# The lead and tile 0's stage of a four-engine transformer kernel in another order: solve input ahead of weight splits, tile 7's scan ahead of the router's maxima

## The reference

```python
x = _layernorm(x + _L0_attn_ref(x, ...))   # delta-rule attention, 4 heads of 32, chunks of 32 tokens
x = _layernorm(x + _L0_ffn_ref(x, ...))    # 8 experts, top two by a router, GELU, hidden 256
x = _layernorm(x + _L1_attn_ref(x, ...))   # gated linear recurrence: a scan over time
x = _layernorm(x + _L1_ffn_ref(x, ...))    # gated silu, two GELU layers of 512, output
```

```python
def body(i, a):
    row = a[..., i, :]
    upd = jnp.einsum('bhnj,bhnjk->bhnk', row, a)
    return a.at[..., i, :].add(upd)
attn = jax.lax.fori_loop(1, c, body, attn)
```

## Time and profile before

| | us |
|---|---|
| median of 3 runs | 868.87 |
| the 3 runs | 862.1, 868.87, 869.66 |
| the profiled execution | 861.58 |
| its span, first to last instruction | 859.7 |

### The profile page before, as it was taken

One profiled execution on the slowest core, in us unless ns is written; L12 is line 12 of the kernel. 1 busy time (PEld: TensorE's weight loads), 2 busy tenths in 40 slices (PEclk: granted clock), 3 DMA queues, 4 the chain that ended last, 5 costly groups with the idle time before them and its releaser, 6 DMA issues.

```text
span 859.7 us, 11901 instructions
## 1 busy us (share of the span) xinstructions
PE 795.8 (93%) x3812; PEld 618.3 (72%) x3812; DVE 614.7 (72%) x1162; ACT 487.4 (57%) x766; POOL 484.4 (56%) x507
## 2 busy tenths in 40 slices
PE   5998699789788999999989999999999999999997
PEld 3776586677467777777767678777877887766775
DVE  2777768897678758776867787768767866777553
ACT  3887246433943574367435744575467447767754
POOL 0039688777546738873785355435553454367343
PEclk9999699789979999999999999999999999999999
DMA  4134615400320110012000400110020000000000
GB/s 135 50 100 122 186 35 148 125 23 0 86 61 26 41 47 1 1 31 69 1 1 2 123 0 2 46 52 0 0 73 25 0 0 13 1 0 1 13 13 13
DMA packets 37903, 35.81 MB, mean 42 GB/s; under 512 B 1632, under 2 KB 30816, under 8 KB 37856
## 3 DMA queue, kind: packets, MB, share of 16 engines
q1 hardware_dynamic: 37856, 35.22, 14.6%
HBM read 21.85 MB, written 13.37 MB: 41 GB/s over the span
## 4 chain that ended last, share of the span: by engine, by line
PE 55%; POOL 14%; issue 8%; DVE 8%; ACT 2%; DMA 0%; DVEq 0%; ACTq 0%; POOLq 0%; SPq 0%
PE bank L439 55%; POOL tpm L1237 4%; POOL tmp L1234 4%; POOL fbl L1293 2%; POOL acc L1301 2%; DVE spread L1530 2%; DVE sexp L1546 1%; DVE yg L1556 1%; DVE fbh L1741 1%; POOL texp L1263 1%; DVE fbl L1739 1%; DVE fah L1798 0%; DMA pack<-pk 0%; DVE ttp L1429 0%; POOL fal L1332 0%
## 5 line engine op out<-in xcount | busy, mean ns | idle before, releaser
L1079 ACT ACTIVATE hf<-bank 128x512 f32<-128x512 f32 x64 | 38.4, 599 | 174.7 <-PE bank L439 169.1
L1293 POOL TENSOR_TENSOR fbl<-hf,fbh 128x512 fp32r<-128x512 f32 x64 | 82.0, 1282 | 70.6 <-DVE fbh L1741 70.6
L1234 POOL TENSOR_TENSOR tmp<-apm,tpm 128x31 f32<-128x31 f32 (+15 forms) x124 | 78.7, 635 | 53.3 <-DVE apm L1420 46.0
L439 PEld LDWEIGHTS bank<-pk,spread 128*128 128x128 f32 x640 | 80.6, 202 | 20.1 <-DVE spread L1530 14.1
L439 PE MATMUL bank<-pk,spread 128*128 128x64 f32 x640 | 83.3, 286 | 9.0 <-DVE spread L1530 8.0
L1324 POOL TENSOR_TENSOR fbl<-hf,fbh 128x512 fp32r<-128x512 f32 x28 | 36.9, 1319 | 89.0 <-DVE fbh L1798 89.0
L1237 POOL TENSOR_TENSOR tpm<-tpm,tmp 128x31 f32<-128x31 f32 (+15 forms) x124 | 78.5, 633 | 9.7
L1301 POOL TENSOR_TENSOR acc<-acc,yg 128x512 f32<-128x512 f32 x48 | 64.6, 1346 | 34.0 <-DVE yg L1556 34.0
L1739 DVE TENSOR_TENSOR fbl<-hf,fbh 128x512 fp32r<-128x512 f32 x64 | 59.6, 931 | 30.5 <-ACT fbh L1085 29.3
L1556 DVE TENSOR_TENSOR yg<-bank,gb 128x512 f32<-128x512 f32 x64 | 43.9, 685 | 35.2 <-PE bank L439 35.1
L439 PE MATMUL bank<-fal,wfh 128*128 128x512 f32 x160 | 67.6, 423 | 0.0
(11 more groups left out here) (240 smaller groups left out, 2220.3 us busy)
## 6 DMA issues: line engine op xcount, KB each, us to landing
pk<-pack SPq DMA_DIRECT2D x7, 1280.0 KB, 7.1
pack<-pk SPq DMA_DIRECT2D x5, 1280.0 KB, 6.8
ws<-in_wf SPq DMA_DIRECT2D x11, 256.0 KB, 3.0
pack<-pk SPq DMA_DIRECT2D x4, 640.0 KB, 4.1
xs<-in_xh SPq DMA_DIRECT2D x8, 262.0 KB, 4.2
xt<-in_xh SPq DMA_DIRECT2D x8, 262.0 KB, 2.9
ws<-in_wm SPq DMA_DIRECT2D x8, 256.0 KB, 2.7
tt<-ttp SPq DMA_DIRECT2D x4, 512.0 KB, 3.1
```

The lines of the kernel that those rows point to most:

```text
L439: return P.matmul(out, lhsT, rhs, start=start, stop=stop, skip_group_check=skip)
L1079: A.activation(hf[:, 0, :], bank[4][:, :], ACT.Gelu).then_inc(S["gelu_done"], 1)
L1234: G.tensor_tensor(m, a, r, ALU.mult).then_inc(S["t_mul"], 1)
L1293: G.tensor_tensor(fbl[:, sl, :], hf[:, 1, :], f32(fbh[:, sh, :]), ALU.subtract)\
```

## The change

No instruction is added or taken away; the order is another on PE, DVE and SP, and three pieces take another buffer.

- Lead, VectorE: tile 1's `gram_rows` and `solve_in(0)` stand ahead of the splits of pieces 2 and 3. In tile 4, `gram_rows` and `solve_out(0)` stand ahead of the splits of pieces 9 and 10; piece 11 moves into `ramp1` and piece 12 to the end of it.
- Lead, TensorE: tile 1's `gram` ahead of `project(2, 2)`; `project(5, 0)` ahead of tile 4's `gram`; through `ramp1` each `project` stands one place earlier.
- `ramp2`, VectorE: the product by beta of pair 1 leaves `solve_out(1)` and becomes `solve_weight(1)` in `dense(0, 1)`, and `store_tt(1)` on SP moves behind `store_pack(6)`. `gate_weights` stands ahead of tile 6's `value_rows` and first `gram_rows`.
- `dense(0, 1)`: splits of two pieces where there were four; pieces 17 and 18 move into `ramp3`.
- `ramp3`: `lru_scan` ahead of `top_two`, `gate_weights` next; `delta_spread` of tile 2 and the split of piece 18 ahead of tile 7's `gram_rows`. TensorE: tile 2's first `delta_wu` and tile 1's first `up` ahead of norm 3's mean product, which takes bank 2 instead of bank 0.

The diff's core:

```diff
-PIECE_BUF = tuple(p % 2 for p in range(NPIECE))
+PIECE_BUF = tuple(p % 2 for p in range(NPIECE - 3)) + (1, 0, 0)
@@ PE, lead
-                    for m in range(3):
-                        project(t + 1, m)
+                    project(t + 1, 0)
+                    project(t + 1, 1)
+                    if t != 1:
+                        project(t + 1, 2)
+                else:
+                    project(t + 1, 0)
                 gram(t, 0)
                 gram(t, 1)
+                if t == 1:
+                    project(t + 1, 2)
@@ PE, ramp3
-                mean_product("3", m, m1, 0)
+                delta_wu(a + 1, 0)
                 pe.wait_ge(S["ws_lo"], WM // PIECE)
                 pe.wait_ge(S["rs_ln"], 2 * (s + 1))
                 up(a, 0)
+                pe.wait_ge(*after("lg_ready", a + 1))
+                mean_product("3", m, m1, 2)
                 gate_turn(a)
                 gram(s, 0)
                 gram(s, 1)
-                var_product("3", m, m2, 1)
-                pe.wait_ge(*after("d3", m + 1))
-                pe.wait_ge(*after("rs3", 2 * m + 1))
+                var_product("3", m, m2, 2)
@@ DVE, lead
-                split_pieces(PIECES[t][:2])
+                if t != 1 and t != LEAD - 1:
+                    split_pieces(PIECES[t][:2])
                 gram_rows(t, 0)
                 gram_rows(t, 1)
-                if t < LEAD - 2 or t == LEAD - 1:
-                    split_pieces(PIECES[t][2:])
                 if t == 1:
                     solve_in(0)
+                    split_pieces(PIECES[t][:2])
+                if t < LEAD - 2:
+                    split_pieces(PIECES[t][2:])
             solve_out(0)
+            split_pieces(PIECES[LEAD - 1][:2])
@@ DVE, ramp3
                 lru_gx(m)
+                split_pieces(PIECES[s][1:2])
                 attention_sum(a)
                 attention_high(a)
                 lru_m(m)
                 attention_low(a)
+                lru_scan(m)
                 top_two(a)
-                lru_scan(m)
+                gate_weights(a)
                 unit_rows(s)
...
-                gate_weights(a)
+                centre("3", m, m1, 2)
                 gate_rows(a)
-                centre("3", m, m1, 0)
                 value_rows(s)
                 beta_rows(s)
+                delta_spread(a + 1, 0)
+                split_pieces(PIECES[s][2:])
                 gram_rows(s, 0)
                 gram_rows(s, 1)
```

More of the change, by code:

```diff
@@ L633, in ramp1 @@
             def ramp1(a, s):
-                project(s, 0)
+                project(s, 1)
                 beta(s)
                 delta_wu(a, 0)
-                project(s, 1)
+                project(s, 2)
                 delta_attn(a, 0)
@@ L640, in ramp1 @@
                 delta_wu(a, 1)
-                project(s, 2)
+                squares(s)
                 delta_attn(a, 1)
@@ L644, in ramp1 @@
                 delta_wu(a, 2)
-                squares(s)
+                project(s + 1, 0)
                 delta_attn(a, 2)
@@ L653, in ramp1 @@
                 gram(s, 1)
-                project(s + 1, 0)
                 beta(s + 1)
@@ L704, in dense @@
                         pe.wait_ge(S["bt_ready"], LEAD + 2)
-                    delta_wu(a, 0)
+                    if not isinstance(m, int) or m != 1:
+                        delta_wu(a, 0)
                 if isinstance(m, int) and m in (0, 1):
@@ L717, in dense @@
                         output_product(f)
+                    if isinstance(m, int) and m == 1 and e == 0:
+                        pe.wait_ge(*after("rs3", 2 * m - 1))
                     if a is not None:
@@ L1720, in dense @@
             def dense(m, a, f, inv=0):
-                if a is not None:
+                if a is not None and (not isinstance(m, int) or m != 1):
                     delta_spread(a, 0)
@@ L1725, in dense @@
                         split_x(NT - 1)
[L1726 to L1728 removed]
+                    if isinstance(m, int) and m == 0 and e == 1:
+                        solve_weight(1)
+                    if isinstance(m, int) and m == 0 and e in (2, 5):
+                        split_pieces((PIECES[NT - 2][2], PIECES[NT - 1][0])[e // 4:e // 4 + 1])
                     if inv == 1 and e == 2:
```

22 lines of the change are left out of this document (11 added, 11 removed).

## The result

The kernel after takes 870.18 us (median of 20 runs, 866.29 to 872.45); the kernel before, on the same chip, 866.20 us (20 runs, 861.82 to 869.66). The ratio is 1.005, with a 95% interval of 1.0034 to 1.0067: 4.0 us slower, where 0.5 us faster was forecast. The measured time lies inside the forecast's range of 866.5 to 870.5 us and 1.8 us from its 868.4, but that is luck: the base, 868.87 us, was the median of three runs and is 2.7 us above that of 20, and the shift has the wrong sign; the two errors partly cancel.

What follows compares the result with a forecast made beforehand. TensorE bounds from 295 us on; before that, GpSimd's solves with VectorE between, then the record's landing and VectorE. Terms -0.4 - 1.9 + 0.4 + 1.4 = -0.5 us on the median gave 868.4 us, range 866.5 to 870.5 (full 858 to 873).

Steps and rivals of the forecast that it cites:

- Lead, the turn: Lead, VectorE's turn of solve 0: held by late xs loads, 0.4 us earlier than 100.64 after the splits' cost.
- Splits beside the solve: Lead: splits of pieces 2 and 3 run slower beside GpSimd's solve, delaying VectorE by none to 2 us, 0.4 taken.
- ramp2, beta's product: ramp2: the product by beta leaves the path behind solve 1, making x 1.9 us earlier.
- From ramp2's `x` to the end of dense(0, 1): gate_weights one place earlier and the moved splits counted 0, except 0.4 us lost to one split.
- +0.4 for the split at expert 5: dense(0, 1): a split now ahead of the low half at 198.28 costs 0 to 0.5 us, 0.4 taken.
- ramp3: ramp3: the record's store goes later, so the first low half of dense(1, 2) starts 1.4 us late (0.9 to 1.9).
- landing term: End of ramp3: the record lands 3.9 us after its later store and releases the first low half at about 254.6.
- 3 us of cover before the landing: ramp3: tile 7's two gram groups could run at half clock without delay, having some 3 us to spare.
- Rival B: Half clock in reordered ramp2 and ramp3 slows two product groups by 1.7 us each: sum +2.9 us, 871.8; chance 0.28.
- Rival A: Lead: late inputs cost nothing, the turn follows solve 0 near 96.1: sum -4.6 us, 864.3; chance 0.22.
- C: The stretch after 295 us absorbs the shift, so nothing changes: 868.9 us; chance 0.05.
- The base and the spread: Whole kernel: shift put on the three-run median 868.87 us; runs at two levels, near 862 and 869.

Runs made afterwards that it cites:

- e1: The kernel before with only the change's new order in the lead and ramp1: 867.32 us, ratio 1.0015 to before.
- e5: The kernel after with ten extra unread TensorE products in ramp2, around the router: 869.79 us, ratio 1.0047 to before.
- e6: The kernel after with nineteen extra unread TensorE products in ramp3: 871.50 us, ratio 1.0069 to before.
- e7: The kernel after with extra unread products at all its longer TensorE waits up to dense(1, 2), the lead's too: 864.53 us, ratio 0.9995 to before.
- e2: The kernel before with only beta's product moved to dense(0, 1), gate_weights one place earlier and tile 1's T store later: 867.09 us, ratio 1.0019.
- e4: The kernel before with only weight pieces 15 to 18 moved (buffers and places of their splits): 870.83 us, ratio 1.0062.
- e3: The kernel before with only ramp3's new order, weight splits as before: 867.71 us, ratio 1.0036.
- e11: The kernel after without the move of weight pieces 15 to 18: 870.92 us, ratio 1.0045 to before.
- e14: The kernel after with twenty-five extra unread products from ramp2's x through dense(0, 1) and nineteen in ramp3, none in the lead: 863.58 us, ratio 0.9969.
- e15: The kernel before with beta's product moved, ramp3's new order, and extra unread products from ramp2's x through ramp3: 860.82 us, ratio 0.9939.
- e8: The kernel before with extra unread products at its longer TensorE waits, the lead's and ramp3's too: 870.03 us, ratio 1.0054.
- e13: The kernel before with extra unread products from ramp2's x through dense(0, 1) only: 863.29 us, ratio 0.9955.

## Why the prediction was wrong, point by point

- **Lead, the turn.** Forecast 0.4 us earlier for the turn (100.2), measured 100.00 (99.40 in after's second profile), with VectorE idle for `xs` for 4.96 and 4.75 us, 5.8 and 6.4 us later than before, and solve 0 done at 96.9. Right, by the mechanism given (the whole lead of this profile began 0.7 us later than before's).
- **Splits beside the solve.** Wrong in what they delay. I counted VectorE's time alone. (My sum there was loose too: three operations a piece at 0.36 us more are 2.2 us for both pieces, not "about 1".) Behind the turn the splits of pieces 9 and 10 now stand beside `texp` and solve 1: `texp`'s first two took 3.00 us instead of 2.47, and solve 1, from its first row to the start of its last, 44.05 us (107.82 to 151.87) instead of 42.80 (from 107.64; the earlier trace rows has its end). A turn 0.6 us earlier has become a solve that ends 1.4 us later; in after's second profile a turn 1.2 us earlier one that ends 0.5 later. e1 shows it alone: the turn 0.7 earlier, `x` 0.6 later. The longer `texp` is in all eight profiles with these splits in place (1.7 us for its second operation, 1.26 to 1.30 without them). That the splits also lengthen solve 1 is not shown: it took 43.6 to 44.05 us in five of the eight, but 43.2 in e5 and e6 and 42.4 in e7, against 42.7 to 43.2 in the profiles without them.
- **ramp2, beta's product.** 1.9 us forecast, 2.4 in e2, and 1.9 carried to the end at an equal clock. Right. With the lead's loss `x` came 0.5 and 1.4 us earlier in after's two profiles, where 2.3 was forecast.
- **From ramp2's `x` to the end of dense(0, 1).** The step that failed: half clock stood at nothing in the sum. I counted +0.4 for the split at expert 5 and put half clock aside as a rival that costs one group of products, 1.7 us. The long stretch has 20 us, and `dense` follows its half clock at 0.4 us per us: 51.1 us in before's first profile, 53.0 in its second, 54.3 and 55.8 in the two of after. That is 3.2 and 4.7 us more than the first, 1.3 and 2.8 more than the second.
- **ramp3.** +1.4 forecast, 2.2 measured (28.2 against 26.0; 1.8 against the second profile's 26.4). The landing term is right (e4, 1.2 us), and another wait of 1 us more decided: half clock on the two `gram` groups, the variance product and the GELU behind it. I had given the grams "3 us of cover before the landing", which held for the record's chain but not for norm 3's, whose last product stands behind both groups.
- **The rivals.** Rival B was right in kind, half clock that the new order brings, and not in its places: its sum, +2.9 us, was for two groups of products, and 4.0 was measured, a good part of it in the long stretch behind `x`. With a chance of 0.28 it stood behind the forecast, because I held that both places had half clock before; they had, but in before's ramp3 it ended (243.3) before the grams began (244.09). Rival A falls: VectorE waited for `xs`. C falls: nothing behind `x3` absorbs the shift (605.2 us from there to the end in before's first profile, 606.5 and 608.8 in after's).
- **The base and the spread.** The two levels of the three runs were the result in small: they go with the two forms of the stretch behind `x` and others like it. I treated them as noise around the median and not as a property that the change could shift. The range's lower end, 866.5, is also 1 us below what its two terms give (0.4 and 0.5 us under 868.4).

What stays open: why after's order so rarely finds the better clock. e2, e3 and e4 each have no run above 0.962, though e4's TensorE does the same as before's up to `x`. Which half-clock stretch an execution has hangs on more than the order of the work, and 12 runs of a kernel do not tell how often. Open too is why e4 costs 3 us more than before at the same mean clock, while after without the same moves (e11) is no faster than with them.

## What to carry to other kernels

Read a spread of several us between executions together with the granted clock of each run: if time follows the clock, compare kernels at an equal clock first, and then ask which order of work gets which clock. In this kernel a wait of TensorE was cheap when wide products stood behind it and small ones, on which others wait, came last; moving the wide work ahead of the wait and leaving the small groups behind traded idle time for half clock (e3, 27.9 us against 26.0). Extra products helped where they held the clock over the small groups (e14, e15) and did harm where they only moved its fall onto them (e8, 30.9 us). So read the profile again after each filling.

## What the runs showed of the hardware that was not expected

- The same kernel, in two executions, had half clock behind `x` for 7 us plus 3.5 us, and for 20.5 us in one piece; the span was 859.7 and 866.8 us.
- The clock fell to half at 154 us in e2 with 0.16 us of idle ahead of the router, 0.45 ahead of the `gram` before it and 0.78 ahead of the product before that. In before's second profile it fell at 155.6 with 2 us of idle ahead of the router. The length of the last wait does not name the places; the same small products stood around both.
- Splits on VectorE beside `texp` slow GpSimd too: its first two operations took 3.0 us instead of 2.5. The splits themselves took 1.63 us (low half) and 2.39 us (cast) beside `texp`, where the same two took 0.69 and 0.42 us with GpSimd idle.
- The store of the record's half landed after 3.8 to 4.0 us nearly everywhere, but after 5.5 us in e6 and 5.4 us in e13, and the low half behind it came that much later (ramp3 27.8 us in e13, 26.0 before). No run tells why.
